# Six extra matmuls per round around the attention energies of a one-core ViT tower kernel

## Time and profile before

| | |
|---|---|
| time, median of three runs | 495.29 us (494.20 to 495.57) |
| profiled execution, its own time | 495.58 us |
| span of the profile, first to last instruction | 493.8 us |
| mean granted TensorE clock | 0.849 |
| TensorE matmul busy | 370.2 us (75%) |
| VectorE, ScalarE, GpSimd busy | 261.3, 203.1, 291.4 us |

### The profile page before, as it was taken

How to read it: one execution, slowest core, us unless ns; L and a number is a source line. 1 busy time by engine, 2 the same in 40 slices (tenths; PEclk the granted TensorE clock), 3 DMA queues, 4 the chain that set the end, 5 groups by cost and what they waited for, 6 DMA issues and landing times.

```text
span 493.8 us, 10106 instructions
## 1 busy us (share of the span) xinstructions
PE 370.2 (75%) x2456; PEld 302.3 (61%) x2457; DVE 261.3 (53%) x1088; ACT 203.1 (41%) x581; POOL 291.4 (59%) x205
## 2 busy tenths in 40 slices
PE   6488989989899786641277879999998898998000
PEld 4465858768677565531156557778887787787000
DVE  0336585957948848378145554444444444444045
ACT  1131143232332332210035556767776767767100
POOL 3000000383682863878587888888888888888533
PEclk9797978969879668655669999999999999999655
DMA  8999996032133861378458999999999999997795
GB/s 242 306 336 306 439 365 212 18 78 63 39 86 82 344 140 20 82 236 293 103 140 153 161 155 155 157 151 155 158 152 155 157 150 155 158 153 120 143 255 177
DMA packets 66303, 85.81 MB, mean 174 GB/s; under 512 B 16840, under 2 KB 61302, under 8 KB 65894
## 3 DMA queue, kind: packets, MB, share of 16 engines
q1 hardware_dynamic: 35734, 59.82, 39.1%
q0 software_dynamic: 29680, 24.95, 34.9%
q10 hardware_dynamic: 864, 0.73, 0.5%
HBM read 45.86 MB, written 39.47 MB: 173 GB/s over the span
## 4 chain that ended last, share of the span: by engine, by line
DVE 20%; PE 19%; issue 19%; DMA 17%; ACT 10%; POOL 8%; ACTq 4%; SPq 1%; DVEq 0%; POOLq 0%
DMA sums_d<-e_sb,tok 13%; POOL rows_d L388 5%; ACT UPW L831 4%; PE B L524 3%; PE B L590 3%; ACTq L274 3%; PE B L509 3%; PE B L432 2%; POOL sums_d L408 2%; ACT e_sb L851 2%; DMA W<-in_brow 2%; DMA W<-sums_d 2%; PE B L564 2%; PE B L466 2%; DVE h L1186 1%
## 5 line engine op out<-in xcount | busy, mean ns | idle before, releaser
L408 POOL DMA_INDIRECT sums_d<-e_sb,tok x112 | 174.0, 1554 | 35.3 <-issue 23.5
L388 POOL DMA_INDIRECT rows_d<-xrow,slot x77 | 105.2, 1366 | 146.0 <-issue 114.7
L685 PEld LDWEIGHTS B<-e_sb,UPW 128*128 128x128 f32 x796 | 105.7, 193 | 10.7 <-issue 5.2
L685 PE MATMUL B<-e_sb,UPW 128*128 128x128 f32 x796 | 109.7, 279 | 0.0
L694 PE MATMUL B<-W,e_sb 128*128 x224 | 73.5, 410 | 20.3 <-DVE e_sb L1177 10.3
L1177 DVE TENSOR_TENSOR e_sb<-e_sb,B 128x128 f32<-128x128 f32 (+1 forms) x112 | 32.2, 288 | 81.1 <-ACT e_sb L839 61.1
L831 ACT COPY UPW<-W 128x512 f32 (+1 forms) x112 | 63.0, 563 | 17.9 <-issue 17.7
L673 PE MATMUL B<-ident,e_sb 128*128 128x128 f32 x224 | 44.8, 283 | 14.1 <-DMA e_sb<-rows_d 13.1
L694 PEld LDWEIGHTS B<-W,e_sb 128*128 128x128 f32 x224 | 34.0, 191 | 33.5 <-issue 33.0
L851 ACT ACTIVATE e_sb<-B,wcol 128x256 f32<-128x256 f32 x112 | 53.0, 473 | 0.2 <-issue 0.2
L1161 DVE COPY e_sb<-B 128x256 f32<-128x256 f32 x112 | 46.9, 419 | 11.2 <-PE B L673 10.4
(11 more groups left out here) (165 smaller groups left out, 470.7 us busy)
## 6 DMA issues: line engine op xcount, KB each, us to landing
e_sb<-rows_d SPq DMA_DIRECT2D x112, 152.5 KB
rows_d<-padrow SPq DMA_DIRECT2D x1, 7320.0 KB, 34.5
W<-in_wx SPq DMA_DIRECT2D x1, 7027.0 KB, 50.4
sums_d<-padrow SPq DMA_DIRECT2D x4, 1408.0 KB, 22.4
W<-in_wx SPq DMA_DIRECT2D x1, 4781.0 KB, 17.2
W<-in_wx SPq DMA_DIRECT2D x1, 4576.0 KB
W<-in_pt SPq DMA_DIRECT2D x4, 666.0 KB, 8.8
sums_d<-e_sb,tok POOLq DMA_INDIRECT x112
```

The source lines that it names most:

```text
L388: pool.indirect_dma_start(rows_d, bass.IndirectOffsetOnAxis(ap=slot[0:n, t, j:j + 1], axis=0), xrow[0:n, t, :], None).then_inc(done, 16)
L408: pool.indirect_dma_start(sums_d[c], bass.IndirectOffsetOnAxis(ap=tok[:, c:c + 1], axis=0), Y[:, c, :], None, compute_op=ALU.add).then_inc ...
L685: mm = pe.matmul(B[2 + u % 2][:, m * P:(m + 1) * P], UPW[:, u % 2, at:at + P], GT[:, u % 2, k, :], start=k == 0, stop=k == KC - 1)
```

## The change

A new function on TensorE issues two matmuls of `ident` (stationary, 128x128) by 256 columns of `w_sgu` into bank 3. Nobody reads what they write. It is called three times in every round that has attention, so 36 matmuls are added in the six rounds. Each call first waits: in round 0 for `bias_ok`, in the others for `h2_ok` of the block before, which the energies waited for already. Nothing is removed or moved.

```diff
+            def stay_busy(b):
+
+                if b:
+                    pe.wait_ge(h2_ok, BLOCKS[b][0])
+                else:
+                    pe.wait_ge(bias_ok, 1)
+                for _ in range(2):
+                    pe.matmul(B[3][:, 0:D], ident[:, :], w_sgu[:, 0, :], start=True, stop=True)
+
...
                 if mid is not None:
+                    stay_busy(mid)
                     energies(mid, tiles[0])
+                    stay_busy(mid)
                 if last is not None:
                     second_transposes(last)
+                if mid is not None:
+                    stay_busy(mid)
                 for t in tiles[1:]:
                     energies(mid, t)
```

## The result

The changed kernel takes **478.48 us**, the median of four runs (476.23 to 480.55), beside 494.75 us for the kernel before (a fourth run, 493.23 us, has joined the three that gave 495.29): a ratio of 0.967, 95% interval 0.961 to 0.974. It is 16.3 us faster.

The account below looks back on a forecast made before the run. TensorE was taken as the bound where its clock falls to 1.2 GHz in the rounds. Gains of 11.8 us, less 2.3 for one fall, plus 0 and 0 for rounds 4 and 5, gave 9.5 us: 485.8 us, range 479.5 to 492.5.

Parts of the forecast that it names:

- The first term: Rounds 0 to 3 with the clock held: gains of 2.5, 2.9, 3.7 and 2.7 us, 11.8 us in all.
- The bound: TensorE sets the pace in the low-clock stretches; at most half their busy time comes back, and what follows shifts along.
- The cost of a pair: Two added matmuls, back to back with other work, take 0.95 us at full clock and 1.9 us at the lower clock.
- Round 2: If the clock holds, the pairs fit waits and the second attend ends at about 109.8 instead of 113.48: gain 3.7 us.
- rounds 1 and 3: With the clock held, gains of 2.9 us in round 1 and 2.7 us in round 3.
- Round 0: The new wait is covered by late masks, the third pair costs part of its 0.95 us: gain 2.5 us.
- I take one fall left in these four, at 2.3 us: In one of rounds 0 to 3 the clock would still fall, taking 2.3 us off the gain.
- Round 4: Clock expected to fall still, one pair covering 0.95 of 3.05 us idle: 2.5 us lost to 3.4 won, taken as 0.
- Round 5: Loss could be 1.7 us; gain capped at 1.8 us by GpSimd's scatters; taken as 0.
- Rival 1: The clock holds in every round, so rounds 4 and 5 win too: 17.0 us gained, 478.3 us; chance 12%.
- Rival 2: Thin operands, not pauses, lower the clock; pairs are paid at 1.2 GHz: 11.5 us lost, 506.8 us; chance 11%.
- The signs: Low clock under 30 us in the first 210, shared_up 1.7 us, second energies about 1.0, shorter GpSimd pause before block 4.

Follow-up runs that it names:

- e1: The full change run again without an edit: 479.9 us, ratio 0.973 to the kernel before.
- e6: The full change with all three pairs on 16-row operands in place of 128, same columns: 502.92 us, ratio 1.016 to the kernel before.
- e7: The full change without its six matmuls of round 5: 480.49 us, ratio 0.972 to the kernel before.
- e4: The full change with only the second pair kept, behind the first energies: 484.71 us, ratio 0.981 to the kernel before.
- e8: The full change without the third pair: 478.22 us, ratio 0.967 to the kernel before.
- e5: The full change with only the third pair kept, behind the second norm's transposes: 492.14 us, ratio 0.990 to the kernel before.
- e2: The full change with its three calls keeping their waits but issuing no matmul: 496.06 us, ratio 1.003 to the kernel before.

## Why the prediction was off

The sum failed in its last three terms, all of which say that the clock would not hold or that its holding would bring nothing: 2.3 us taken off for a fall in rounds 0 to 3, where none came; 0 for round 4, where 4.9 us were won (2.5 with a fall); 0 for round 5, where 1.8 were. The first term, 11.8 us, measured 13.2.

**The bound: right.** The low stretches were taken for TensorE's path, half of their busy time for the most that can come back, and the rest of the round for a chain that shifts as a whole. The account above has the gains of rounds 0 to 4 carried on. One reading of the earlier trace rows was wrong, and nothing in the sum hangs on it: the clock does not stand at 9 "to the end" from 260 us on, its last three slices are 6, 5 and 5.

**The cost of a pair: right.** 0.95 and 1.9 were taken. In round 2 the third pair takes 0.98 us from its start to the next start (96.74 to 97.72; its row says 1.04, that of a pair behind other work 1.13); at the lower clock it is 1.87 (e1: 153.50 to 155.37, row 2.08).

**Round 2: 3.7 forecast, 4.2 measured**, rounds 1 and 3 2.9 and 2.7 against 3.5 and 3.4. The sequence is the one foretold: the first pair inside the wait for ScalarE, the second ahead of the transposes, the third under the masks. What was sized too high was the part of the pairs that lies on the path behind the shorter pauses of rounds 1 and 3: of half the low stretch, 4.6 and 4.9 us, 1.1 and 1.5 us were lost there, not 1.7 and 2.2. Round 0: 2.5 forecast, 2.1 measured to the next energies. The first four thus sum to 13.2 instead of 11.8.

**"I take one fall left in these four, at 2.3 us": wrong.** This is one of the two steps that failed. In the two profiles of the full change rounds 0 to 3 have no fall. The worry was the thin L495 ahead of the first pair; the dense pairs behind it were enough.

**Round 4: "I expect the clock to fall there still ... I take 0": half wrong, and the other step that failed.** It fell in one profile of two. But the loss foreseen of 2.5 us did not come even then: the clock was back before route and shared_up. That the dense pairs brought it back is what e6 speaks for, where thin pairs in the same round left it low for 13.7 us instead of 6.8; from round 4's energies to round 5's it is 3.6 us won in the one and, with the fall, 165.11 to 194.41 (29.30) against 151.74 to 178.56 (26.82), 2.5 us in the other. Up to block 3's first scatter, which is what counts for the end, it is 27.29 us before, 22.37 after and 24.81 with the fall: 4.9 and 2.5 us won. This is the largest term that was mis-sized.

**Round 5: "a gain is capped ... at most 1.8 us": the cap was right, to take 0 was not.** From block 3's first scatter to block 4's it is 25.10 us before and 23.28 after: 1.82 us. e7 shows that the pace is GpSimd's there.

**Rival 1 said all this** and was given 12%: 17.0 us, 478.3. Its argument, three dense pairs within 5 us, should have weighed more than the pauses of round 4. The prediction calls its lower end of 479.5 us "most of rival 1", although rival 1's own figure lies below it. That this figure meets the median of 478.48 so closely is in part luck: in the two profiled executions its terms of 11.8, 3.4 and 1.8 us measured 13.2, 4.9 and 1.8, with 0.9 given back, 19.0 in all, and the executions of the full change spread over 7.5 us (476.23 to 483.69).

**Rival 2 had half of the cause.** "Thin operands and not pauses bring it down" was given 11%, and the argument against it was that the 4 us ahead of round 2's fall were more than half idle. With thin pairs in the pauses (e6) the clock falls all the same, so thin work does bring it down; what rival 2 had wrong is that dense pairs would not help. The prediction put dense work into the pauses without telling the two apart; the runs show that the rows matter.

**The signs.** These came: shared_up takes 1.75 us, the second energies 1.02 to 1.17 in rounds 1 to 4, and GpSimd's pause shrank to 0.30. "Under 30 us" of low clock in the first 210 did not: it is 35.8. The sign was badly set. Its 61 us are the six stretches of the earlier trace rows, and three more (from 16.8, 180.6 and 208.0 us on) make it 73.7 before.

**The page that spoke against it.** The Trainium skill, TensorE: Matmul & The Clock Gate, section "HAM oscillation — how this bites in real kernels", puts the fall down to waits that are long against the bursts. The trace does not agree here: with thin pairs the clock falls without a pause longer than 0.42 us in the 4.75 us ahead (e6), and with full rows it holds in rounds 1 to 3. The prediction took from that rule that the change would bring nothing there, and 11.1 us were won in these three rounds; but e6 shows too that filling the pauses by itself, with thin matmuls, brings nothing.

## What to carry to other kernels

Where the granted clock falls at the same place in every round, look at what TensorE does ahead of it, thin operands as well as pauses, and ask whether what stands behind the fall is on the path. Matmuls without use can then be worth more than they cost, if they fill all rows, start inside waits that are there anyway, and stand ahead of the point where the clock falls. Find the place where another queue takes over (here the scatters); beyond it a faster TensorE brings next to nothing (e7: 1.5 us on shared_up were 0.35 us at the scatters).

## What the runs showed of the hardware

- A matmul with 16 rows of operands takes about as long as one with 128 (rows of 1.02 and 1.13 us for the group of four at 2.4 GHz) and does not keep the clock up (0.83 over 36 to 188 us against 0.98); that it counts for so little was half expected from L495, and that a TensorE busy 91% of the time loses its clock was not (e6).
- Dense work at or just ahead of the fall mostly went with a shorter low stretch: 3.4 us with the second pair alone in rounds 1 to 3 (e4; in rounds 2 and 3 the pair had run ahead of the fall), 6.8 in e1's round 4 and 3.4 in e8's against 13.7 before. It did not always: in e5's rounds 1 and 2 a pair at the lower clock left it at 10.2 us.
- A pause stands ahead of one of GpSimd's last scatters in all 14 profiles, 2.27 (e6) to 7.17 us (e2) long, whose end the trace gives to no engine. Between the two profiles of the full change it accounts for 2.3 us, and nothing here shows its cause.
